# Attention of an audio tower: score, P^T and z accumulators in single PSUM banks, scores three tiles ahead, head pairs written out

## What is computed

```python
q = jnp.einsum('bqd,hdm->bqhm', x, W_Q) + b_Q        # k and v likewise
scores = jnp.einsum('bqhm,bkhm->bhqk', q, k) / 8
scores = jnp.where(causal, scores, -100000.0)
pattern = jax.nn.softmax(scores, axis=-1)
z = jnp.einsum('bhqk,bkhm->bqhm', pattern, v)
attn_out = jnp.einsum('bqhm,hmd->bqd', z, W_O) + b_O
```

## Time and profile before

| | us |
|---|---|
| three runs | 1682.6, 1685.71, 1689.65 (median 1685.71) |
| the profiled execution | 1688.44 |
| its span, first to last instruction | 1686.7 |
| mean granted TensorE clock | 0.931 of 2.4 GHz |

### The profile page before, as it was taken

One profiled execution on the slowest core, in us unless ns is written; L12 is line 12 of the kernel. 1 busy time (PEld: TensorE's weight loads), 2 busy tenths in 40 slices (PEclk: granted clock), 3 DMA queues, 4 the chain that ended last, 5 costly groups with the idle time before them and its releaser, 6 DMA issues.

```text
span 1686.7 us, 31187 instructions
## 1 busy us (share of the span) xinstructions
PE 1461.1 (87%) x10191; PEld 977.8 (58%) x10192; DVE 1091.1 (65%) x2482; ACT 772.9 (46%) x1490; POOL 413.7 (25%) x431
## 2 busy tenths in 40 slices
PE   5987799999987799999986899989876999959997
PEld 3443477786433577784443677784433777745665
DVE  6988545457987455567897455559885555583553
ACT  2654455543654455524563555516643555432332
POOL 3000233313000234312000343302002456722222
PEclk7999799997989799997998999989989999968999
DMA  5996122210000122201000222200001453212221
GB/s 126 351 351 200 34 46 59 50 34 34 8 0 1 38 64 46 64 11 40 1 1 0 66 46 64 46 2 29 0 1 27 108 129 88 62 37 67 63 63 32
DMA packets 112867, 104.96 MB, mean 62 GB/s; under 512 B 55133, under 2 KB 103322, under 8 KB 112786
## 3 DMA queue, kind: packets, MB, share of 16 engines
q1 hardware_dynamic: 83570, 55.32, 13.7%
q10 hardware_dynamic: 25744, 39.62, 7.1%
q0 software_dynamic: 3472, 8.97, 1.6%
HBM read 29.57 MB, written 47.40 MB: 46 GB/s over the span
## 4 chain that ended last, share of the span: by engine, by line
PE 46%; DVE 32%; issue 12%; ACT 5%; POOL 3%; SPq 2%; DMA 1%; POOLq 0%; DVEq 0%; ACTq 0%
PE ps L1912 12%; DVE arena L1323 10%; PE ps L1963 6%; DVE arena L1321 6%; PE ps L1886 5%; PE ps L1898 5%; PE ps L1854 5%; DVE bn L1481 4%; PE ps L2010 2%; DVE arena L1350 2%; PE ps L1861 2%; ACT arena L1029 1%; SPq L588 1%; POOL out L920 1%; DMA arena<-arena 1%
## 5 line engine op out<-in xcount | busy, mean ns | idle before, releaser
L1963 PE MATMUL ps<-arena,cwt 128*128 128x504 f16 (+2 forms) x1776 | 389.2, 378 | 40.3 <-DVE arena L1321 36.6
L1963 PEld LDWEIGHTS ps<-arena,cwt 128*128 128x128 f16 x1776 | 172.2, 101 | 257.3 <-DVE arena L1321 39.9
L1342 DVE TENSOR_REDUCE nmax<-ps 128x1 f32<-128x128 f32 (+5 forms) x288 | 176.8, 614 | 176.7 <-PE ps L1889 176.6
L1912 PE MATMUL ps<-arena 128*128 128x64 f32 (+2 forms) x2016 | 259.1, 269 | 8.2 <-DVE arena L1350 4.8
L1912 PEld LDWEIGHTS ps<-arena 128*128 128x128 f32 (+2 forms) x2016 | 240.6, 188 | 25.0 <-issue 13.9
L1323 DVE TENSOR_TENSOR arena<-arena 128x1008 f16<-128x1008 f32 (+4 forms) x200 | 227.0, 1135 | 6.9
L1350 DVE COPY arena<-ps 128x512 f32<-128x512 f32 (+4 forms) x288 | 155.6, 540 | 84.3 <-PE ps L1898 79.2
L988 ACT ACTIVATE arena<-ps,nmax 128x128 f32<-128x128 f32 (+5 forms) x288 | 180.3, 626 | 39.4 <-DVE nmax L1342 38.7
L1886 PE MATMUL ps<-arena 128*128 128x512 f16 (+6 forms) x780 | 163.8, 313 | 29.7 <-ACT arena L1029 16.4
L1061 ACT ACTIVATE arena<-ps 128x1008 f32<-128x1008 f32 (+1 forms) x112 | 96.0, 866 | 178.5 <-PE ps L1963 178.5
L1898 PE MATMUL ps<-ident,arena 128*128 128x128 f32 (+2 forms) x1008 | 165.0, 281 | 11.0 <-ACT arena L1029 6.0
(11 more groups left out here) (290 smaller groups left out, 2263.9 us busy)
## 6 DMA issues: line engine op xcount, KB each, us to landing
slot_scratch<-empty_slot ACTq DMA_DIRECT2D x1, 38692.5 KB, 120.6
arena<-arena SPq DMA_DIRECT2D x96, 187.5 KB, 3.0
arena<-arena SPq DMA_DIRECT2D x96, 93.8 KB, 2.3
arena<-in_L_ffn_w SPq DMA_DIRECT2D x16, 288.0 KB, 5.5
arena<-in_L_ffn_w SPq DMA_DIRECT2D x8, 576.0 KB, 5.9
arena<-slot_scratch SPq DMA_DIRECT2D x31, 96.5 KB, 1.9
arena<-slot_scratch SPq DMA_DIRECT2D x31, 96.0 KB, 1.9
xa<-in_x POOLq DMA_DIRECT2D x4, 468.8 KB, 4.8
```

The costliest lines, as they stand in the source:

```text
L1342: v.reduce_max(nmax[0:m, k_:k_ + 1], slot(g)[0:m, 0:128 * i + m], AX.X, negate=True).then_inc(S["smax_done"], 1)
L1912: last = t.matmul(slot(g)[0:m, Z_AT:Z_AT + DH], probt[k % 2][0:kk, c, 0:m], vt[0:kk, c, DH * hh:DH * hh + DH], start=c == 0, stop=c == i)
L1963: last = t.matmul(bank(g, k)[:, 0:c * PITCH].rearrange("p (r c) -> p r c", c=PITCH), cwt[layer][:, w, tap, :], parts[x][:, f:f + 2 * c - 1 ...
```

## The change

- TensorE's, ScalarE's and VectorE's orders of a pair stand as three written lists. S3 stands for step 3's score, S12 to S14 for steps 0 to 2 of the next pair; MX is the maximum, EX the exp, CP and CA the copies of P^T, RC the reciprocal, ZC, QC, KC, VC and TC the copies of z, q, k, v and z^T.
- Scores are three tiles ahead instead of two; the next pair's S 0 comes behind Z 8. Three scores of a batch, not two, use unstacked halves.
- Banks 0 to 3 serve S (one bank for tiles 0 to 3, two for tiles 4 and 5), Q, K, V and ZT (two each); banks 4 to 7 serve PT; z goes to the first columns of its PT's first bank. A job waits for the last reader of each of its banks (`TAKERS`).
- `prob` has four buffers (the fourth lies on `xnt0`), `probt` three (the third on `xnt1`).
- No loop over pairs: all engines have six pairs written out for each batch, waits are for constants.
- In the last batch SyncE and GpSimd no longer load and split weights that no pair uses (pair 0 to 2 of a batch that doesn't come).

```diff
-PROBS = 3
-Z_AT = TT * 128
-def pair_jobs(last):
-    jobs = []
-    for k in range(STEPS):
-        ahead = k + 2
-        if ahead < STEPS:
-            jobs.append(("s", (ahead,), (ACT_ENGINE,)))
-        elif ahead == STEPS + 1 and not last:
-            jobs.append(("s", (STEPS,), (ACT_ENGINE,)))
-        if k in (TT - 1, TT) and not last:
-            jobs.append(("q" if k == TT - 1 else "k", (), (ACT_ENGINE,)))
-        jobs.append(("pt", (k,), (DVE_ENGINE, ACT_ENGINE) if TILE_ORDER[k % TT] >= 4 else (DVE_ENGINE,)))
-        if k:
-            jobs.append(("z", (k - 1,), (ACT_ENGINE,)))
...
+PE_ORDER = ("S3 PT0 S4 PT1 Z0 S5 PT2 Z1 S6 PT3 Z2 S7 PT4 Z3 S8 Q PT5 Z4 S9 K PT6 Z5 S10 PT7 Z6 S11 PT8 Z7 PT9 Z8 "
+            "S12 PT10 Z9 S13 PT11 Z10 S14 Z11 V ZT").split()
+ACT_ORDER_OF_PAIR = ("EX3 EX4 CA1 ZC0 EX5 ZC1 EX6 CA3 ZC2 EX7 ZC3 EX8 QC ZC4 EX9 KC ZC5 EX10 CA7 ZC6 EX11 ZC7 CA9 ZC8 EX12 "
+                     "ZC9 EX13 ZC10 EX14 ZC11 VC").split()
+DVE_ORDER = ("MX3 CP0 RC0 MX4 CP1 RC1 MX5 CP2 RC2 MX6 CP3 RC3 MX7 CP4 RC4 MX8 CP5 RC5 MX9 CP6 RC6 MX10 CP7 RC7 "
+             "MX11 CP8 RC8 CP9 RC9 MX12 CP10 RC10 MX13 CP11 RC11 MX14 TC").split()
+PROBS, PROBTS = 4, 3
+S_BANKS, P_BANKS = 4, 4
...
+def attention_banks():
+    banks, at_s, at_p = {}, 0, 0
+    for kind, p, k in ATT_PE:
+        if kind == "PT":
+            n = 2 if tile_of(k) >= 4 else 1
+            banks[kind, p, k] = [S_BANKS + (at_p + j) % P_BANKS for j in range(n)]
+            at_p += n
+        elif kind == "Z":
+            banks[kind, p, k] = banks["PT", p, k][:1]
+        else:
+            n = 1 if kind == "S" and tile_of(k) < 4 else 2
+            if at_s + n > S_BANKS:
+                at_s = 0
+            banks[kind, p, k] = list(range(at_s, at_s + n))
+            at_s = (at_s + n) % S_BANKS
+    return banks
...
+def last_takers():
+    holder, takers = {}, {}
+    for job in ATT_PE:
+        takers[job] = [taken_by(*holder[x], x) for x in BANKS[job] if x in holder]
+        for x in BANKS[job]:
+            holder[x] = job
+    return takers
...
-        prob = [take(TT * 128) for _ in range(PROBS)]
-        probt = [take(TT * 128).rearrange("p (t c) -> p t c", c=128) for _ in range(2)]
+        prob = [take(TT * 128) for _ in range(3)] + [xnt0]
+        probt = [a.rearrange("p (t c) -> p t c", c=128) for a in (take(TT * 128), take(TT * 128), xnt1)]
...
-            for pr in range(PAIRS - 1):
-                stack_heads(PAIR, b, pr)
-                wait(sp, "w_split", PAIR, 1, b, pr)
-                load_pair((pr + 3) % PAIRS)
-                load_experts(range(2 + 2 * pr, min(4 + 2 * pr, EXPERTS)))
+            for p in range(1, PAIRS):
+                stack_heads(p, b)
+                if p + 2 < PAIRS:
+                    wait(sp, "w_split", ATT, p, b)
+                    load_pair(p + 2)
+                load_experts(range(2 * p, min(2 + 2 * p, EXPERTS)))
...
-                split_weights(PAIR, BATCH - 1, pr)
-                w2_high(pr)
+                if p + 1 < PAIRS:
+                    split_weights(ATT, BATCH - 1, p)
+                w2_high(p - 1)
...
-                with act.Fori(0, PAIRS - 1) as pr:
-                    for g, n, kind, args in jobs_of(PAIR):
-                        attention_job(PAIR, g, n, kind, args, b, pr)
-                for g, n, kind, args in jobs_of(LAST_PAIR):
-                    attention_job(LAST_PAIR, g, n, kind, args, b)
+                for kind, p, k in ATT_ACT:
+                    attention_step(kind, p, k, b)
...
+            def banks_free(job, b):
+                takers = TAKERS[job]
+                by_act = [ACT_NTH[x] for x in takers if x[0] not in ("CP", "TC")]
+                by_dve = [DVE_NTH[x] for x in takers if x[0] in ("CP", "TC")]
+                if by_act:
+                    wait(pe, "act_freed", ATT, max(by_act), b)
+                if by_dve:
+                    wait(pe, "dve_freed", ATT, max(by_dve), b)
...
-                        if k in (2, STEPS):
-                            wait(pe, "head0_stacked", phase, 64 if k == STEPS else 0, b, pr)
-                        if k == TT:
-                            wait(pe, "head1_stacked", phase, 0, b, pr)
+                        wait(pe, f"head{hh}_stacked", ATT, 64 * (p + 1), b)
...
-                        last = t.matmul(slot(g)[0:m, Z_AT:Z_AT + DH], probt[k % 2][0:kk, c, 0:m],
+                        last = t.matmul(bank_at(BANKS[job][0])[0:m, 0:DH], probt[(STEPS * p + k) % PROBTS][0:kk, c, 0:m],
                                         vt[0:kk, c, DH * hh:DH * hh + DH], start=c == 0, stop=c == i)
```

More of the change, by code:

```diff
@@ L221 @@
[L221 to L233, removed]
@@ L248, in split_unit_of, with at @@
     return (layer, next(c for c in range(len(NORM_CHUNKS[layer])) if row < sum(NORM_CHUNKS[layer][:c + 1])))
[L251 to L255, removed]
+def at(sem, phase, k, b=None):
+    setup, tower, att, post, last_post = COUNTS[sem]
     if phase == SETUP:
         return k
-    period = before_last + last_pair + post
+    period = tower + att + post
     if phase == MOE:
         return setup + BATCH * period - post + last_post + k
[L261 to L288, removed]
+    return b * period + setup + {TOWER: 0, ATT: tower}.get(phase, tower + att) + k
 def freed(phase, engine, n):
-    if engine == ACT_ENGINE and phase in (PAIR, LAST_PAIR):
-        return ACT_ORDER[phase].index(n) + 1
     return sum(engine in job[2] for job in JOBS[phase][:n + 1])
@@ new lines, in banks_free, with attention_step @@
+            def banks_free(job, b):
[6 more added lines that the diff above has]
+                    wait(pe, "dve_freed", ATT, max(by_dve), b)
+            def attention_step(kind, p, k, b):
+                job = kind, p, k
+                i, hh = tile_of(k), k // TT
+                m = tile_rows(i)
+                banks_free(job, b)
+                if kind in "QKV":
+                    wait(pe, "w_split", ATT, p - 1, b)
+                    last = project(kind.lower(), [bank_at(x) for x in BANKS[job]])
+                elif kind == "S":
+                    places = banks_at(job)
+                    if p == 0 and k < FIRST_SCORES:
@@ L1917, in attention_job @@
-                    wait(pe, "act_freed", phase, freed(phase, ACT_ENGINE, done), b, pr)
-                    for i in range(TT):
-                        m = tile_rows(i)
-                        last = t.transpose(slot(g)[:, 128 * i:128 * i + m], z[0:m, i, :], ident[0:m, 0:m])
+                    assert kind == "ZT"
+                    wait(pe, "act_freed", ATT, ACT_NTH["ZC", p, STEPS - 1], b)
+                    for n in range(TT):
+                        m = tile_rows(n)
+                        last = t.transpose(banks_at(job)[:, 128 * n:128 * n + m], z[0:m, n, :], ident[0:m, 0:m])
```

478 lines of the change are left out of this document (226 added, 252 removed).

## The result

The changed kernel takes 1777.56 us (median of four runs, 1758.59 to 1778.26), the kernel before 1685.2 beside it on the same chip. The ratio is 1.052, 95% interval 1.0445 to 1.0592: slower, by some 92 us, where the forecast was 43. The profiled execution of after took 1778.26 us. The shortest of the four, 1758.59, is also the one with the highest mean granted clock, 0.917 against 0.891 to 0.894 in the others.

What follows compares the result with a forecast made beforehand. TensorE, busy for 87% of the span, was taken as the engine to follow. Terms 27 + 6 + 6.6 - 7 + 0 + 10 = +43 us, from the median 1685.71 us, gave 1728 us; range 1702 to 1752.

Steps and rivals of the forecast that it cites:

- K to S12: TensorE, k product to next pair's first score: 9.8 us, with a new 2.3 us wait for the stacks' DMA.
- Rivals A and B: A: stacks still in time, 1673 us, chance 0.10; B: stacks bind but waits elsewhere vanish, 1669 us, chance 0.05.
- The steady pair: Attention pairs between a batch's first and last: 30.1 us each, +1.7; 16 of them give +27 us.
- ZT to Z1: TensorE, from the z^T step to z 1: 4.88 us, against 3.35 of TensorE's work in it.
- Z1 to K: TensorE, from z 1 to the k product: 8.78 us, of which 8.19 is work.
- The clock: Attention, behind the new wait: half clock for 3 us in a third of 20 pairs, +10 us, bounds 0 and 34.
- rival C: Attention: the clock falls in nearly every pair, 43 + 24, 1752 us; chance 0.17.
- four first pairs: First pair of each batch: as a steady one, less 0.2 us; +1.5 each, four times +6 us.
- four last pairs: Last pair of each batch: S10 waits 1.2 us for S9's exp; ends 1.65 us later, +6.6 us in four.
- tail: Last batch, after attention: without POOL's weight splitting beside them, VectorE's six additions fall from 9.34 to 1.68 us, -7 us.
- Nothing for the buffers: More P and P^T buffers: no wait in the timeline is for a P buffer; nothing, at most one copy, 0.7 us.
- Nothing for the code: Pairs written out: jumps gone against more code to read; taken as 0, bounds -22 and +33 us.

Runs made afterwards that it cites:

- the two kernels that keep the clock: The changed kernel with ten (1728.65 us) or four (1721.2 us) useless matmuls put on TensorE ahead of the wait for the stacks.
- the kernel with four useless matmuls: The changed kernel with four useless matmuls of 512 columns on TensorE ahead of each pair's wait for the stacks: 1721.2 us, ratio 1.0190.
- the kernel without the transfer in the path: The changed kernel with every pair's score tiles 12 to 14 made from q's and k's parts: 1679.53 us; with three P, two P^T buffers 1694.27 us.
- two moves of list items: The changed kernel with q's product behind S6, k's behind S8, and S12 behind PT10 and Z9: 1669.64 us, ratio 0.9926.

## Why the prediction was right and wrong

**The chain and the wait: right.** K to S12 was put at 9.8 us with 2.3 us of wait; 10.05 and 2.39 came out in 18 of 20 pairs, a little more in two, with the DMA as the releaser. The chain was priced step by step from rows of before: ScalarE's copy, two passes on GpSimd, the issue, the landing. Rivals A and B are refuted by the trace, since the wait is there in each of the 20 pairs and the pair at full clock is longer than before.

**The steady pair: right.** 30.1 us without the clock's part; 30.16 and 30.17 in the two kernels that keep the clock. In after, ZT to Z1 (303.54 to 308.42) was 4.88 us, as walked, and Z1 to K 8.74 against 8.78.

**The clock: this is the step that failed.** The prediction counted "half clock for 3 us in a third of 20 pairs at 1.5 us each: +10; bounds 0 and 34". The runs show it in all 20 pairs, for 7 us in the mean, at 2.6 us each: 51 us. A third of the pairs and 3 us were guesses, and no row gave them. The sum has an error too: 20 pairs at 1.5 us each are 30, not 34, so rival C, priced with the 34, stands 4 us too high. Rival C had the frequency right, at a chance of 0.17, but its price was one short stretch.

The evidence was in the earlier trace rows, and I misread it. The stretch from 203.30 to 210.10 holds the wait of 2.06 us itself, so TensorE worked at half clock for 4.7 us behind it and not for 6.8. The other three batches of the kernel before, whose first score waits 2.06 to 2.08 us as well:

```profile
571.90:578.70 6.80, 5.12 (x24) 4.19 (x25) 3.52 (x9) 2.91 (x8) 2.69 (x4) 0.50 0.59 144
940.50:943.90 3.40, 3.40 (x18) 2.59 (x16) 2.39 (x6) 1.28 (x5) 0.67 (x1) 0.50 0.50 118
1305.80:1309.20 3.40, 3.40 (x17) 2.77 (x16) 2.14 (x5) 0.95 (x4) 0.82 (x1) 0.50 0.55 126
```

Work that takes 4.74, 5.12, 3.40 and 3.40 us at half clock takes half of that at full clock: a loss of 2.1 us in the mean and 2.6 at most. The clock fell in four waits of four, so these rows gave 42 to 51 us for 20 pairs as the main case; 51 came out. The same reckoning on the changed kernel, 127 us of work at half clock, gives 64 us, so it is no more than an estimate: some of the loss seems to be taken up by other waits.
By the Trainium skill (TensorE: Matmul & The Clock Gate, HAM oscillation) a loop can pay the clock gate in each turn, when each turn waits for a DMA. The trace agrees: 20 waits of 2.35 to 3.53 us, 20 stretches at 0.50.

**The rest of the sum.** Held against the kernel with four useless matmuls, whose span is 34.0 us over that of before, it went like this:

| term | predicted | measured |
|---|---|---|
| 16 steady pairs | +27 | +27.7 (1.73 each) |
| four first pairs | +6 | +5 |
| four last pairs | +6.6 | +1.2 (22.46 against 22.16, ZT to ZT) |
| tail | -7 | -8 |
| towers and setup | 0 | +5 |
| half clock left in this kernel | (in the clock's term) | +3 |
| sum | +33 | +34 |

Two errors cancel here, and that the sum agrees is luck. The last pairs were over-priced: the wait of 1.2 us for the exp of S9 ahead of S10 is not there. In the last pair of batch 0 of the same trace S10 starts without idle time, right behind Z5:

```profile
368.54 1.00 PE L1885 MATMUL ps<-arena 128*128 128x64 f32 x8
369.38 0.49 PE L1865 MATMUL ps<-arena 128*128 128x384 f16 x2
```

And the towers, which the change does not touch, took 5 us more in this trace; 7 in that of the changed kernel. That part I could not trace to a cause; it lies within what they vary by.

**Nothing for the buffers: right as a sum, wrong as a reason.** I wrote that no wait of before is for a buffer. True, but it was the wrong timeline to ask. In the new order the fourth P and the third P^T buffer hold off 20 us, 1.0 us a pair where my bound was "one copy, 0.7 us"; in the kernel without the transfer in the path it is 0.71. The walk of the new pair had no wait for a buffer, so the sum was not hurt.

**Nothing for the code: right within the measurement.** 0.2 us of each loop turn, ahead of the z^T copy, was in my stretches by name; whether the rest of the 0.57 was, I did not work out. Against written-out code in the old order the new order alone costs 2.3 us a pair, not 1.7.

**The range.** 1702 to 1752 missed by 26 us at the top. 20 of these are the clock's bound: 51 us and the 3 of the table, against 34. The other 6 are what is left of smaller terms (the towers +7, the longer way from K to S12 +3, the last pairs -5). The sign was right.

## What to carry to other kernels

A new wait on the engine that bounds has two prices: its own length, and the slow clock behind it, which here was as large (2.6 us against a wait of 2.4). If a trace shows waits of that size and what the clock did behind them, price each new wait by these rows as the main case: half of the time that TensorE was busy at half clock, without the wait itself. When a step depends on a transfer, move its source earlier and its user later until there is margin for the slowest landing: two moves of list items turned a loss of 5.2% into a gain of 0.7%. And part the change before you credit it: here the gain was that of written-out loops and of work left out, not of the new order.

## What the runs showed that was not expected

- Of the waits ahead of S12, those of up to 1.0 us left the clock alone in all pairs but one (0.70 us at 1075.60, with q and k earlier), and every one of 2.35 us and more in the changed kernel came with half clock. Between them it depends on more than the wait: 1.4 us behind four useless matmuls kept the clock in 18 of 20 pairs, while 1.1 us (at 960.9) in the kernel with q and k earlier came with half clock, and 1.7 us (at 687.0) in the kernel with S12 alone moved did not.
- Useless work of 1.0 us in a wait bought back 56 us, the difference of the medians 1777.56 and 1721.2. Ten matmuls bought less than four (1728.65): seven steady pairs of that kernel take 31 us, as transfers landed later, and its attention stages take 734.2 us against 730.1. The other half of the 7.5 us between the medians I did not trace.
- A buffer can bind two engines away: with three buffers of P and not four the copy of k came later, because it stands behind an exp in ScalarE's queue.
